# Queries and keys split by Pool from a float copy; TensorE's repeated waits left out

## The reference

```
xn = layernorm(x)
s = recurrent(xn)                       # projections, convolution, scan, output projection
h1 = rmsnorm(xn, ln1); q, k, v = h1 @ Wq.T, h1 @ Wk.T, h1 @ Wv.T        # 16 heads of 32
attn = softmax(causal(q k^T / sqrt(32))) v @ Wo.T
mod = 0.1 * tanh(attn @ A)              # A is 512 x 16
h = rmsnorm(xn, ln2)
gate = silu(h @ W_in_base.T + mod * (h @ A) @ B)
y = xn + (gate * (h @ W_up_base.T)) @ W_down.T
out = x + s * silu(y)
```

## Time and profile before

| | us |
|---|---|
| median of 3 runs | 2517.82 (2512.28 to 2519.99) |
| profiled execution, its own time | 2519.63 |
| its span | 2517.6 |
| PE busy | 2443.1 (97%) |
| DVE busy | 1364.4 (54%) |
| ACT busy | 1048.8 (42%) |
| POOL busy | 469.7 (19%) |

### The profile page before, as it was taken

One profiled execution on the slowest core, in us unless ns is written; L12 is line 12 of the kernel. 1 busy time (PEld: TensorE's weight loads), 2 busy tenths in 40 slices (PEclk: granted clock), 3 DMA queues, 4 the chain that ended last, 5 costly groups with the idle time before them and its releaser, 6 DMA issues.

```text
span 2517.6 us, 38024 instructions
## 1 busy us (share of the span) xinstructions
PE 2443.1 (97%) x14039; PEld 1980.1 (79%) x14039; DVE 1364.4 (54%) x2860; ACT 1048.8 (42%) x1791; POOL 469.7 (19%) x430
## 2 busy tenths in 40 slices
PE   7999999999999899999999899999999999999998
PEld 5878878878778677777777688888888788888887
DVE  7856657667655587888888742111214322222223
ACT  6444444544544476777777621111112211111112
POOL 4000000000001254444444500000000202222222
PEclk9999999999999999999998999999999999999999
DMA  4000100000003676676666221001113312222212
GB/s 144 18 34 1 34 26 9 34 18 17 18 17 106 206 219 190 197 206 197 191 189 197 65 98 51 26 26 51 51 51 138 114 46 101 97 100 96 101 63 84
DMA packets 107738, 228.09 MB, mean 91 GB/s; under 512 B 15360, under 2 KB 16384, under 8 KB 101392
## 3 DMA queue, kind: packets, MB, share of 16 engines
q1 hardware_dynamic: 105056, 225.31, 27.9%
q10 hardware_dynamic: 2496, 0.29, 0.1%
HBM read 149.77 MB, written 75.50 MB: 89 GB/s over the span
## 4 chain that ended last, share of the span: by engine, by line
PE 87%; DVE 7%; issue 3%; ACT 2%; DMA 1%; SPq 0%; DVEq 0%; POOL 0%; ACTq 0%
PE PS L72 14%; PE PS L74 13%; PE PS L73 13%; PE PS L2219 4%; PE PS L2220 4%; PE PS L2221 4%; PE PS L1744 3%; PE PS L1705 3%; PE PS L812 2%; PE PS L811 2%; PE PS L813 2%; PE PS L1723 2%; PE PS L1706 2%; PE PS L1707 2%; DVE PS L1908 1%
## 5 line engine op out<-in xcount | busy, mean ns | idle before, releaser
L2288 DVE TENSOR_TENSOR SG<-SG,PS 128x512 f32<-128x512 f32 x124 | 85.3, 688 | 643.9 <-PE PS L74 642.6
L74 PE MATMUL PS<-FH,GU 128*128 128x512 f32 x992 | 388.3, 391 | 0.0
L73 PE MATMUL PS<-FL,GU 128*128 128x512 f32 x992 | 387.5, 391 | 0.0
L72 PE MATMUL PS<-FH,GU 128*128 128x512 f32 x992 | 387.3, 390 | 0.0
L1908 DVE CUSTOM_DVE_ANT_0 PS<-PS,MK 128x512 f32<-128x512 f32 (+3 forms) x512 | 244.7, 504 | 73.5 <-PE PS L1723 72.2
L2258 ACT ACTIVATE SG<-PS 128x512 f32<-128x512 f32 x124 | 74.5, 601 | 466.6 <-PE PS L2195 466.5
L2324 POOL TENSOR_SCALAR XN<-XT,MEAN,RSTD 128x512 f32<-128x512 f32 x32 | 68.7, 2146 | 941.9 <-DMA M<-m_scratch 941.9
L1844 ACT ACTIVATE PF<-PS 128x512 f32<-128x512 f32 (+1 forms) x384 | 201.0, 528 | 93.0 <-PE PS L1748 60.5
L2261 ACT CAST GH<-SG 128x512 fp32r<-128x512 f32 x124 | 77.1, 622 | 350.4 <-DVE SG L2288 350.4
L73 PEld LDWEIGHTS PS<-FL,GU 128*128 128x128 f32 x992 | 186.5, 188 | 41.1
L72 PEld LDWEIGHTS PS<-FH,GU 128*128 128x128 f32 x992 | 186.4, 188 | 40.7
(11 more groups left out here) (295 smaller groups left out, 5224.9 us busy)
## 6 DMA issues: line engine op xcount, KB each, us to landing
qk_scratch<-QT SPq DMA_DIRECT2D x128, 256.0 KB, 4.6
QS<-qk_scratch SPq DMA_DIRECT2D x96, 256.0 KB, 4.0
KS<-qk_scratch SPq DMA_DIRECT2D x96, 256.0 KB, 4.0
FH<-rh_scratch SPq DMA_DIRECT2D x16, 1024.0 KB, 5.4
FL<-rl_scratch SPq DMA_DIRECT2D x16, 1024.0 KB, 7.3
XF<-in_x_dram SPq DMA_DIRECT2D x32, 256.0 KB, 3.9
s_scratch<-ZS SPq DMA_DIRECT2D x8, 1024.0 KB, 4.3
rh_scratch<-RH SPq DMA_DIRECT2D x8, 1024.0 KB, 9.5
```

Source lines behind the costliest of these rows:

```text
L72: pe.matmul(o, lh(k), xh(k), start=open_ and k == 0, stop=False, skip_group_check=True)
L73: pe.matmul(o, lh(k), xl(k), start=False, stop=False, skip_group_check=True)
L74: last = pe.matmul(o, ll(k), xh(k), start=False, stop=close and k == nk - 1, skip_group_check=True)
```

## The change

Three things are changed in the attention stage. ACT copies the projected bank to a new float tile QF (one for queries, one for keys) and signals a_qf; it waits for the split two pieces before (a_ql), no longer for the DMA. POOL makes from QF the high part by a cast and the low part by a subtraction, and it now waits for the DMA out of QT (a_qo). The bank is free with a_qf. DVE's subtraction is gone. The place of `project_low` in the table of steps stays, so that it stands at the same point of the list, but in POOL's stream.

PE's waits on semaphores that an earlier instruction of its stream has already waited for are left out: in the recurrent branch s_xl for all but the first of a block, a_q, a_k and a_nm for all but the first of 12 thirds, a_w for all but the very first, and in the FFN a_th and a_mo for all but the first column of a block (and the column with q = 4), and for the whole second half.

```diff
-                pe.wait_ge(s_xl, 4 * b + 4)
+                if m == 0:
+                    pe.wait_ge(s_xl, 4 * b + 4)
...
+        QF = [sb(at_, f"QF{n}", [128, S]) for n in range(2)]
...
             elif kind == "project" and how[1] == 0:
-                key, free = (kind, a, how[0]), (a_ql, 2 * a + how[0] + 1)
+                key, free = (kind, a, how[0]), (a_qf, 2 * a + how[0] + 1)
...
-                    pe.wait_ge(a_qk[0], qk_landed(w))
-                    pe.wait_ge(a_qk[1], qk_landed(w))
+                    if a % 12 == 0:
+                        pe.wait_ge(a_qk[0], qk_landed(w))
+                        pe.wait_ge(a_qk[1], qk_landed(w))
...
-                    pe.wait_ge(a_nm, 16 * w + 16)
-                    pe.wait_ge(a_w, 96)
+                    if a == 0:
+                        pe.wait_ge(a_w, 96)
+                    if a % 12 == 0:
+                        pe.wait_ge(a_nm, 16 * w + 16)
...
                     act.wait_ge(a_pj, 2 * a + n + 1)
-                    if a >= 2:
-                        act.wait_ge(a_qo[n], 32 * (a - 1))
-                    act.copy(QT[n][a % 2][0][:, :], bank01(kind, a, n)[:, :]).then_inc(a_qh, 1)
+                    if a:
+                        act.wait_ge(a_ql, 2 * (a - 1) + n + 1)
+                    act.copy(QF[n][:, :], bank01(kind, a, n)[:, :]).then_inc(a_qf, 1)
...
-                elif kind == "project_low":
-                    dve.wait_ge(a_qh, 2 * a + how + 1)
-                    dve.tensor_tensor(QT[how][a % 2][1][:, :], bank01("project", a, how)[:, :], f32(QT[how][a % 2][0][:, :]),
-                                      ALU.subtract).then_inc(a_ql, 1)
...
+                elif kind == "project_low":
+                    hi, lo = QT[how][a % 2]
+                    pool.wait_ge(a_qf, 2 * a + how + 1)
+                    if a >= 2:
+                        pool.wait_ge(a_qo[how], 32 * (a - 1))
+                    pool.tensor_copy(hi[:, :], QF[how][:, :]).then_inc(a_qh, 1)
+                    pool.wait_ge(a_qh, 2 * a + how + 1)
+                    pool.tensor_tensor(lo[:, :], QF[how][:, :], f32(hi[:, :]), ALU.subtract).then_inc(a_ql, 1)
...
-                    pe.wait_ge(a_th, 3 * b + 3)
-                    pe.wait_ge(a_mo, 2 * b + 2)
+                    if q < 8 * NB and (f == 0 or q == EARLY):
+                        pe.wait_ge(a_th, 3 * b + 3)
+                        pe.wait_ge(a_mo, 2 * b + 2)
```

More of the change, by code:

```diff
@@ L1304, in build @@
         qk_d = nc.dram_tensor("qk_scratch", [2, 4, 2, 128, S], F32R, kind="Internal").ap()
-        (a_xs, a_tr, a_rh, a_rl, a_pj, a_qh, a_ql, a_vl, a_vh, a_v1, a_vp, a_ha, a_lg, a_mx, a_ti, a_ni, a_wt, a_ex, a_ph,
+        (a_xs, a_tr, a_rh, a_rl, a_pj, a_qf, a_qh, a_ql, a_vl, a_vh, a_v1, a_vp, a_ha, a_lg, a_mx, a_ti, a_ni, a_wt, a_ex, a_ph,
          a_rm, a_rp, a_pv, a_ao, a_nu, a_sm, a_tm, a_th, a_mo) = sems(
-            "a_xs a_tr a_rh a_rl a_pj a_qh a_ql a_vl a_vh a_v1 a_vp a_ha a_lg a_mx a_ti a_ni a_wt a_ex a_ph "
+            "a_xs a_tr a_rh a_rl a_pj a_qf a_qh a_ql a_vl a_vh a_v1 a_vp a_ha a_lg a_mx a_ti a_ni a_wt a_ex a_ph "
             "a_rm a_rp a_pv a_ao a_nu a_sm a_tm a_th a_mo")
```

## The result

The changed kernel takes 2538.80 us (median of 5 runs, 2533.66 to 2542.32); the kernel before took 2513.81 beside it (5 runs, 2512.28 to 2519.99). The ratio is 1.0093, 95% interval 1.0080 to 1.0107: 23 us slower (the two medians are 25 us apart; the ratio goes by all the runs). The forecast was slower at 2531 with a range of 2509 to 2551, against 2517.82 then, a loss of 13 us. Direction and range hold; the loss is near twice what the sum gave.

What follows compares the result with a forecast made beforehand. TensorE was taken as the pacing engine, busy 541.23 of 570 us in the attention stage. Terms 0 - 4.1 + 12.6 + 4 = +12.5 us on 2519.63 gave 2532, forecast as 2531 against the median 2517.82; range 2509 to 2551.

Steps and rivals of the forecast that it cites:

- Waits, 0 us: Leaving out TensorE's waits on semaphores reached long before gains 0 us, bound -12.4 us for FFN and attention stage.
- DVE, -4.1 us: In the attention stage, of 64 subtractions taken from DVE only six pieces of 0.68 us are on the path: -4.1 us.
- POOL, +12.6 us: Casts and subtractions delay POOL's remainders in the attention stage: 7 periods x (0.3 + 0.2 + 1.3) = +12.6 us.
- the one replayed period: Heads 48 to 63 of the attention stage, with three tight places in POOL's queue: heads 57, 53 and 61.
- Head 61: TensorE's mixed step waits 1.0 to 3.0 us for POOL's remainder, 1.9 taken; net 0 to 2.3, 1.3 taken.
- the other two places: Remainders of heads 57 and 53 come late by 0 to 0.5 (0.3 taken) and 0 to 0.4 us (0.2 taken).
- The lock, 0 us on the path: POOL's SBUF reads block DVE's remainder in the attention stage: 15 us on DVE against 43 lost, 0 on the path.
- The clock, +4 us: Half clock after TensorE stands near 3 us in the attention stage: up to 24 us, one or two taken, +4.
- Rival E: Clock falls in each attention period as head 61 stands about 3 us: 2557 at worst, 2545 likelier; chance 0.14.
- A: The forecast itself: POOL is late in the attention stage; 2531 us, own range 2523 to 2541; chance 0.45.
- The sign given for E: Half-clock stretches behind each of TensorE's waits in the attention stage.
- A's signs: One 1 to 3 us wait a period for POOL's remainder; POOL 395 to 430 us; L1913 above 1.4; pace 0.232 unchanged.

Runs made afterwards that it cites:

- the split alone: The changed kernel with all of TensorE's waits put back, leaving only the split by POOL: ratio 1.0091 to the kernel before.
- the waits alone: The kernel before with nothing changed but PE's repeated waits left out: ratio 1.0001.
- the filled kernel: The changed kernel with 40 small matmuls ahead of TensorE's wait in the mixed step of heads 13, 29, ... 109: ratio 1.0064.
- no pair: The changed kernel with one four-column memset replacing each POOL cast and subtraction from the fifth split on, ACT writing the high part: ratio 0.9984.
- two replacements: Four memsets replace POOL's cast and subtraction, in the changed kernel with each period's last split one third later (1.0037) and in its own order (1.0072).
- the best order with 64 pairs: The changed kernel with splits moved behind the remainders they stood ahead of, the last of a period at third 52: ratio 1.0012.

## Why the prediction was right, and where it fell short

*Waits, 0 us.* Right (1.0001, within 3 us). That the slow pace follows the operands was argued, not tested.

*DVE, -4.1 us.* Right in size (-4.0) and in its place: the subtraction that is in the chain once a period is the only one that counts, since moving it alone brings all of it (0.9979). The kind holds too: the stand is 0.60 us shorter, against 0.68 predicted for each of six.

*POOL, +12.6 us.* The mechanism holds to the instruction, and so does the one replayed period; the term is too small. Head 61 was to stand 1.0 to 3.0 us, 1.9 taken; it stood 2.2. Of TensorE's 1.0 us for DVE, 0.6 was to go; it went from 1.00 to 0.57. Taken 0.3 and 0.2 for the other two places: one shows a wait of 0.16 to 0.17 a period, the other none. The scaling took 2.07 us.

On the scaling the prediction read one row (1.31 us at 1102.23) as not held. DVE's remainder takes 1.22 us undisturbed, and the trace of the kernel before shows what the 0.09 are:

```profile
1203.28 2.07 POOL L1967 TENSOR_SCALAR STGB<-STGB,MEAN,RMS 128x512 f32<-128x512 f32 x1
1204.84 1.22 DVE L1913 TENSOR_TENSOR PL<-PF,PH 128x1024 f16<-128x1024 f32 x1
...
1243.62 2.08 POOL L1967 TENSOR_SCALAR STGB<-STGB,MEAN,RMS 128x512 f32<-128x512 f32 x1
1243.94 1.51 DVE L1913 TENSOR_TENSOR PL<-PF,PH 128x1024 f16<-128x1024 f32 x1
```

Of thirteen remainders issued inside a scaling there, seven came 0.33 to 0.53 us after its start; this time and their delay make 0.62 us in each. The six others came 1.56 us after it or later and were not delayed. So the scaling holds DVE for its first 0.62 us only. In the changed kernel nine came 0.64 us or more behind the start and took 1.22 us each (six more came in its last 0.03 us and were held by the sum behind it); one of the nine:

```profile
1221.26 2.08 POOL L1968 TENSOR_SCALAR STGB<-STGB,MEAN,RMS 128x512 f32<-128x512 f32 x1
1221.91 1.22 DVE L1914 TENSOR_TENSOR PL<-PF,PH 128x1024 f16<-128x1024 f32 x1
```

The Trainium skill's rule (SBUF — State Buffer, Who interferes with whom), read in full, would have it wait for the scaling's end. The casts and subtractions agree with it, the scaling does so for 0.62 of its 2.07 us; the sum went by the rows, rightly.

What the term missed is the first period. I multiplied one replayed period by seven. In the first one POOL waits 4.82 us for a row of x (before: 4.81), the remainder is queued behind that, and TensorE stood 2.5 and 3.1 us more; the period is 11.2 us longer in this pair of executions, and 6.1 longer (77.8 against 71.7) in the split alone against the waits alone. By the filled kernel, which has the queue and no half clock from 940 to 1360, a period takes 72.9 us on average (73.5, 72.6, 72.7, 73.1, 72.7) against 69.8 with no pair. That is 3.1, where the term had 1.8, and more than the stand of 2.2 itself; what makes up the rest is not shown.

*The lock, 0 us on the path.* Wrong. DVE lost 7.8 us in L1914 where I expected 15, but two replacements show about 5 us of the pair's reads in the time of the kernel, near the limit of what the runs resolve. The step that failed is "against 43 that it lost": DVE was relieved over the whole stage and slowed where it paces.

*The clock, +4 us.* The size was too small: a half-clock stretch came with each of the seven waits, where one or two were expected; summed over the clock's records the profiled executions have 82.8 us at half clock against 58.4. It is worth 7 us by the filled kernel. The row that I went by, full clock behind a stand of 1.00 us at 1151.11, is one of several: behind the same stands at 1221.5 and 1293.1 the kernel before has 3.4 us at half clock (0.50 from 1222.4 to 1225.8).

Together: queue and lock 20 us (the filled kernel's 1.0064 against 0.9984 with no pair), less DVE's 4, and the clock's 7: the 23 measured. The three come from three ratios and add up by construction. Where the forecast had +12.5, POOL is the term that was too small. Rival E, the clock at each period, describes what happened better than A did; its price of 2545 to 2557 was too high, because it took half of every half-clock stretch as lost. (2545 is what its sum gives when the clock's part alone is halved; half of all of it is 2537. The forecast's own last step, 2532 less 1.8, gives 2530 and not 2531.) The sign given for E, half clock behind each wait, came true beside A's wait of 1 to 3 us a period; two of A's signs were just missed, L1914's mean above 1.4 us (1393 ns) and POOL at 395 to 430 us (392.92).

What stays open: why the stretch of half clock is 3.4 us behind one wait and 6.8 behind another of the same 2.2 us; how the remaining 7 us of the best order with 64 pairs divide between lock and queue; and why the first period loses most, of which each version has one trace.

## What to carry to other kernels

Before moving work to an engine that looks idle, replay its stream in order around the instructions that others wait for, in the first period as well as in a middle one: the pair of 2 us ahead of a result with 1.0 us of slack (1150.46 against 1151.46) cost more in each period (3.1 us) than its subtractions gave back (0.6). Ask which of the repeated instructions stands on the path; here moving one in eight, placed behind the tight stretch, had the whole gain (0.9979 against 1.0093 for moving all). And price a stand of TensorE of some 2 us with the clock behind it, though below half of the time at half clock: here 7 us, give or take 5, of 20.8.

## What the runs showed of the hardware

Each of the stands of TensorE of 2.2 us was followed by half clock, 3.4 or 6.8 us of it, and where they were filled with small matmuls there was none. Stands of 1.0 us were followed by it in some periods only. With four memsets for the pair in the changed order, none of the thirteen two-input subtractions of DVE that were issued inside one of them was held (1.22 us each); with casts and subtractions of POOL that read SBUF their mean rose from 1323 ns in the kernel before to 1393 in the changed one. POOL's scaling of 128x512 held such a subtraction in its first 0.62 us alone, but a scaling issued while the subtraction ran was stretched from 2.07 to 3.05 us. 1056 satisfied wait instructions fewer changed nothing that can be measured (1.0001, 0.9989 to 1.0012).
